# Who copies an attention group's last transposed probabilities, and where one row tile of the output projection begins

## The reference

```
q = rms_norm(layernorm(x));  k = rms_norm(ctx);  v = ctx          # 16 q heads, 4 k/v heads of width 32
scores = einsum('bgnqd,bgkd->bgnqk', rope(q), rope(k)) / sqrt(32)
attn = softmax(where(causal, scores, -1e30))
out = einsum('bgnqk,bgkd->bgnqd', attn, v)
x = x + out.reshape(B, T, C) @ w_out.T
x = x + ffn0(layernorm(x))
x = x + softmax(layernorm_rows(similarity(layernorm(x), ctx)))    # its parts run inside the next batch's attention
x = x + experts(layernorm(x))
```

## Time and profile before

| | us |
|---|---|
| median of 3 runs (1294.71 to 1297.57) | 1295.18 |
| the profiled execution | 1294.44 |
| its span | 1292.6 |
| busy in the span: PE, DVE, ACT, POOL | 1197.4 (93%), 736.1 (57%), 523.0 (40%), 444.1 (34%) |
| chain that ended last | PE 71%, DVE 14%, ACT 6%, DMA 3% |

### The profile page before, as it was taken

One profiled execution on the slowest core, in us unless ns is written; L12 is line 12 of the kernel. 1 busy time (PEld: TensorE's weight loads), 2 busy tenths in 40 slices (PEclk: granted clock), 3 DMA queues, 4 the chain that ended last, 5 costly groups with the idle time before them and its releaser, 6 DMA issues.

```text
span 1292.6 us, 19512 instructions
## 1 busy us (share of the span) xinstructions
PE 1197.4 (93%) x6575; PEld 866.9 (67%) x6575; DVE 736.1 (57%) x1498; ACT 523.0 (40%) x1189; POOL 444.1 (34%) x508
## 2 busy tenths in 40 slices
PE   4999999989999998999999899999899999999990
PEld 3667777667777766777776677777456666666650
DVE  7957665686788579677867967554712222222220
ACT  4865222775412278541227853222333323233320
POOL 1431233431123442113353211121165555555530
PEclk8999999999999999999999999999999999999995
DMA  8013230002232000323200012642789999999847
GB/s 294 2 68 107 98 107 34 1 1 110 100 138 102 35 1 12 120 78 138 102 34 1 34 69 78 238 171 75 306 254 357 358 348 356 342 345 351 228 55 141
DMA packets 45907, 187.04 MB, mean 145 GB/s; under 512 B 6717, under 2 KB 9789, under 8 KB 31365
## 3 DMA queue, kind: packets, MB, share of 16 engines
q1 hardware_dynamic: 30964, 146.18, 30.0%
q0 software_dynamic: 14864, 39.85, 13.6%
HBM read 155.31 MB, written 34.90 MB: 147 GB/s over the span
## 4 chain that ended last, share of the span: by engine, by line
PE 71%; DVE 14%; ACT 6%; DMA 3%; issue 2%; POOL 2%; DVEq 0%; SPq 0%; POOLq 0%; ACTq 0%
PE PS L2547 14%; PE PS L1971 10%; PE PS L1973 10%; PE PS L1972 10%; PE PS L2563 4%; ACT P L871 4%; DVE NM L1401 3%; PE PS L2567 3%; PE PS L2059 3%; PE PS L2078 2%; PE PS L2537 2%; PE PS L1990 2%; DMA WRAW<-in_ffn 2%; PE PS L2364 1%; PE PS L2363 1%
## 5 line engine op out<-in xcount | busy, mean ns | idle before, releaser
L2547 PE MATMUL PS<-WE,XGT 128*128 128x384 f32 x512 | 192.7, 499 | 1.5 <-DVE HM L1948 0.8
L698 POOL CAST HH<-HID 128x512 fp32r<-128x512 f32 x44 | 37.2, 846 | 330.4 <-DVE HID L1777 317.2
L997 ACT ACTIVATE WHI<-WRAW 128x1280 fp32r<-128x1280 f32 x44 | 56.1, 1274 | 223.9 <-DMA WRAW<-in_ffn 223.9
L1971 PE MATMUL PS<-XTH,WHI 128*128 128x512 f32 x352 | 141.1, 401 | 3.3 <-DVE WLO L1720 3.3
L871 ACT ACTIVATE P<-PS,NM 128x512 f32<-128x512 f32 (+3 forms) x256 | 131.8, 532 | 25.8 <-DVE NM L1401 24.8
L1973 PE MATMUL PS<-XTH,WLO 128*128 128x512 f32 x352 | 138.2, 393 | 0.0
L1972 PE MATMUL PS<-XTL,WHI 128*128 128x512 f32 x352 | 138.0, 392 | 0.0
L2547 PEld LDWEIGHTS PS<-WE,XGT 128*128 128x128 f32 x512 | 87.1, 190 | 56.7 <-issue 21.5
L1955 DVE COPY HMT<-PS 128x256 f32<-128x256 f32 x64 | 27.2, 425 | 163.8 <-PE PS L2556 163.8
L2059 PE MATMUL PS<-ident,P 128*128 128x128 f32 x640 | 94.6, 280 | 18.5 <-ACT P L871 8.4
L1401 DVE TENSOR_REDUCE NM<-PS 128x2 f32<-128x1024 f32 (+2 forms) x96 | 98.8, 1040 | 20.4 <-PE PS L1980 20.1
(11 more groups left out here) (337 smaller groups left out, 2696.1 us busy)
## 6 DMA issues: line engine op xcount, KB each, us to landing
WE<-in_we SPq DMA_DIRECT2D x64, 1152.0 KB, 8.1
WRAW<-in_ffn SPq DMA_DIRECT2D x44, 1060.0 KB, 4.9
acc<-HN SPq DMA_DIRECT2D x17, 256.0 KB, 7.0
XIN<-in_x SPq DMA_DIRECT2D x4, 1024.0 KB, 5.5
out<-X SPq DMA_DIRECT2D x4, 1024.0 KB, 4.5
out<-acc POOLq DMA_DIRECT2D x1, 4096.0 KB, 22.9
hx<-HN SPq DMA_DIRECT2D x3, 1152.0 KB, 4.5
CTX<-in_ctx SPq DMA_DIRECT2D x4, 256.0 KB, 2.8
```

Of the source, the lines that this page charges most:

```text
L997: act.activation(WHI[slot][:, 0:WD], WRAW[slot][:, 0:WD], ACT.Copy).then_inc(S["wg_hi"], 1)
L1971: pe.matmul(dst, a[0], b_[0], start=first, stop=False, **kw)
L2547: mm = pe.matmul(bank(2 + s % 2, 0, 2 * F1), XGT[s % 2][:, k, :], WE[s][:, k * 2 * F1:(k + 1) * 2 * F1], start=(k == 0), stop=(k == KC - 1))
```

## The change

The table of who copies what is altered, and the engines' programs with it:

- Tile 0 (all four heads) of every group is copied by ScalarE instead of VectorE, behind ScalarE's copies of tile 1 and the fifth stack.
- Tile 2, head 3 of groups 0 to 2 is copied by VectorE instead of ScalarE, behind head 2. In the last group VectorE made that copy already; there tile 2, head 0 goes from VectorE to ScalarE.
- In group 0 of the batches with a tail, the first query stack is copied by VectorE instead of ScalarE, and one row-statistics instruction (L1343) moves behind the tile-2 copies.
- In group 2 with a tail, ScalarE takes the exponentials of y row tile 2 behind the tile-2 copy instead of ahead of its score exponentials.
- In batches 1 to 3, TensorE does the first two head groups of row tile 1's projection inside the last group: three matmuls between the transposes of tile 1 and tile 0, three between the context transposes and the value product. It waits there for two split outputs.

```diff
@@ turning_order
-            order += [("P", g, 2, 0, 1, "d"), ("P", g, 2, 1, 1, "a")]
+            order += [("P", g, 2, 0, 1, "a" if g == G - 1 else "d"), ("P", g, 2, 1, 1, "a")]
...
-                order += [("stack", g + 1, 0, "d"), ("stack", g + 1, 1, "a")]
-            order += [("P", g, 2, 2, 1, "d"), ("P", g, 2, 3, 1, "d" if g == G - 1 else "a")]
+                order += [("stack", g + 1, 0, "d"), ("stack", g + 1, 1, "d" if tail and g == 0 else "a")]
+            order += [("P", g, 2, 2, 1, "d"), ("P", g, 2, 3, 1, "d")]
...
-            order += [("P", g, 0, 0, 4, "d")]
+            order += [("P", g, 0, 0, 4, "a")]
@@ ScalarE, attention
-                    if tail and g == 2:
-                        exp_y(2)
                     exps(a, g, 3)
                     if tail and g == 0:
                         normed_T("xT3", 1)
+                    if g == G - 1:
+                        turned(g, 2, 0)
                     turned(g, 2, 1)
+                    if tail and g == 2:
+                        exp_y(2)
...
                     exps(a, g, 4)
-                    if g < G - 1:
+                    if g < G - 1 and not (tail and g == 0):
                         stack(g + 1, 1, QST[0])
                     exps(a, g, 5)
-                    if g < G - 1:
-                        turned(g, 2, 3)
...
                     if g < G - 1:
                         stack(g + 1, 4, QST[3])
+                    turned(g, 0, 0, 4)
@@ VectorE, attention
-                    turned(g, 2, 0)
+                    if g < G - 1:
+                        turned(g, 2, 0)
...
                     if g < G - 1:
                         stack(g + 1, 0, KST)
-                    if rows_in:
-                        n = stats_x2(b, 3)
+                        if rows_in:
+                            stack(g + 1, 1, QST[0])
                     if sims:
                         peak(0)
                     turned(g, 2, 2)
-                    if g == G - 1:
-                        turned(g, 2, 3)
+                    turned(g, 2, 3)
+                    if rows_in:
+                        n = stats_x2(b, 3)
...
                     divisors(g)
-                    turned(g, 0, 0, 4)
@@ TensorE, attention (projected_out moves ahead of the loop, unchanged)
                     turn(g, 1, 2, 2)
                     if g < G - 1:
                         stack(g + 1, 4)
+                    if tail and g == G - 1:
+                        pe.wait_ge(S["oT_lo"], 1 + (G - 1) * a + 2)
+                        projected_out(1, 0, 1)
                     turn(g, 0, 0, 4)
...
                         context_T()
-                        if not tail:
+                        if tail:
+                            projected_out(1, 1, 2)
+                        else:
                             router_sums()
                     times_v(g)
...
-                    projected_out(t, 0, KC - 1)
+                    projected_out(t, 2 if tail and t == 1 else 0, KC - 1)
```

More of the change, by code:

```diff
@@ L881, in turned @@
                     src = bank(turns.bank("P", g, t, n0, nh), 0, nh * (t + 1) * P)
-                    src = src.rearrange("p (n j q) -> p n j q", n=nh, q=P) if nh > 1 else src.rearrange(
+                    src = src.rearrange("p (n j q) -> p n j q", n=nh, q=P) if t == 1 else src.rearrange(
                         "p (j q) -> p j q", q=P)
@@ L2170, in context_T, with projected_out @@
                     mm.then_inc(S["ctxT_ps"], 1)
+                def projected_out(t, k0, k1):
+                    sl = slice(t * P, (t + 1) * P)
+                    for k in range(k0, k1):
+                        mm = three(bank(2 + t), (OTH[:, k, sl], OTL[:, k, sl]), (woH[:, k, :], woL[:, k, :]),
+                                   k == 0, k == KC - 1)
+                    return mm
                 for g in range(G):
@@ L2230, in attention @@
                         keys_out()
-                def projected_out(t, k0, k1):
-                    sl = slice(t * P, (t + 1) * P)
-                    for k in range(k0, k1):
-                        mm = three(bank(2 + t), (OTH[:, k, sl], OTL[:, k, sl]), (woH[:, k, :], woL[:, k, :]),
-                                   k == 0, k == KC - 1)
-                    return mm
                 pe.wait_ge(S["oT_lo"], 1 + (G - 1) * (a + 1))
```

## The result

The changed kernel took 1283.99 us (median of 4 runs, 1283.72 to 1285.12), the kernel before beside it 1295.27 (1294.71 to 1297.57): a ratio of 0.9911, 95% interval 0.9894 to 0.9928, or 11.3 us less. The prediction was 1286.2 (1282.8 to 1291.5), faster. The profiled execution after took 1285.12 us with a span of 1283.3, which is 9.3 less than the span before. The forecast against the profiled execution was 9.0, but that these two agree so closely is chance, as the table shows: a start that came 1.4 later and a batch that gained 1.5 more than forecast nearly cancel.

The account below looks back on a forecast made before the run. TensorE bounds the FFN; in attention three engines hand over to each other, leaving short waits. 3 x (1.1 + 0.95 + 1.05) - 0.3 = 9.0 us off 1294.44 gives 1285.4, at the median 1286.2 (1282.8 to 1291.5).

Parts of the forecast that it names:

- Groups 0 to 1: Batches 1 to 3, transition from group 0: TensorE's waits for ScalarE copies go, scores start earlier; gain 1.1 us a batch.
- Groups 2 to 3: Batches 1 to 3: earlier transposes and VectorE maxima free of the tile-0 copy, staying early afterwards; gain 0.95 us a batch.
- Groups 1 to 2: Transition where VectorE waits for a similarity product: the extra copy ends just before it lands; 0 (0 to 0.1 lost).
- Projection: Last group, batches 1 to 3: six matmuls (1.4 us) saved behind the value product, 0.3 paid ahead; gain 1.05 a batch.
- Batch 0: First batch: VectorE's added copy meets GpSimd's subtraction; 0.6 and 0.2 us lost, group 2 gains 0.5; loss 0.3.
- more comes back: Rival: early projection partly fills the idle before batch 2's low TensorE clock; without the dip, with upper ends, 1283; chance 0.08.
- gain is cut: Rival: later gates in the group transitions of batches 1 to 3 take back part of the gain; 1290.1 us, chance 0.20.
- VectorE's row becomes the gate: Rival: copies added on VectorE delay the second stack copy in all transitions of batches 1 to 3; 1298.5 us, chance 0.05.
- The early step: Last group, batches 1 to 3: rival that transposes behind the early projection slip 0.7 us, leaving 0.4 a batch; 1288, no separate chance.

Follow-up runs that it names:

- e3: Kernel before with only the tile-2, head-3 copy of groups 0 to 2 moved to VectorE: 1290.89 us, ratio 0.9975.
- e4: Kernel before with only the tile-0 copy of every group moved to ScalarE: 1290.59 us, ratio 0.9974.
- e6: Changed kernel with the first query stack of group 0, batches 1 to 3, copied by ScalarE again: 1284.78 us.
- e9: Changed kernel without the early projection, three useless projection matmuls filling the idle ahead of the last group's tile-0 transposes in batches 1 to 3: 1286.60 us, ratio 0.9934.
- e1: Kernel before with only the early projection in the last group of batches 1 to 3, all copies as before: 1289.95 us, ratio 0.9967.
- e2: Changed kernel without the early projection, all copies moved: 1288.47 us, ratio 0.9960.
- e7: Changed kernel with batch 0's first query products on VectorE moved behind the second stack copy and the tile-1 copy, groups 0 and 1: 1282.55 us.
- e5: Changed kernel with batch 0's tile-2, head-3 copy of groups 0 and 1 given back to ScalarE: 1282.78 us.
- e8: Changed kernel with one more projection step inside the last group of batches 1 to 3, ahead of the tile-1 transposes: 1281.99 us.

## Why the prediction was right, point by point

- **Groups 0 to 1, 1.1 a batch:** measured 1.08, 1.10 and 1.06. Each gate on the way lay within 0.03 us of where the prediction put it. e3, e4 and e6 share it out: 0.47 for head 3, 0.12 for tile 0, 0.48 for the stack copy. The prediction named the XTF copy as the next gate; that is where the change stopped gaining.
- **Groups 2 to 3, 0.95 a batch:** 0.56 up to group 2's value product (forecast 0.6) and the rest behind it. In e9, where no projection blurs it, V2 to V3 is 0.50 shorter, and the stage of batch 1 is 2.00 shorter than before, 0.92 of it behind group 0. The claim that VectorE's row, once early, stays early to the last group's maxima held: ScalarE's wait of 1.47 us shrank to 0.46, and the exponentials of tile 1 came 0.91 earlier, counted from group 1's value product.
- **Groups 1 to 2, 0:** 23.13 and 23.12 in batch 1. In batch 2 it went from 23.46 to 23.11. This 0.35 was not foreseen. Both profiles of before and e1 have it, e2 and e4 don't, e3 has half; its cause was not followed.
- **Projection, 1.05 a batch:** saved behind 1.33 (forecast 1.4), paid ahead 0.24 in e1 and 0.38 in the changed kernel against e9 (forecast 0.3 to 0.4). For the whole stage, e1 against before gives 1.02 and 0.98 in batches 1 and 3, the changed kernel against e9 1.07, 0.97 and 0.78 in the three.
- **Batch 0, loss 0.3:** measured 0.27 at group 0 (0.2 forecast), 0.44 at group 1 (0.6), -0.74 at group 2 (-0.5), +0.18 in the last group (0, cause not followed): 0.15 in all. Group 1 was over-sized because the new copy runs beside the subtraction's first part, so the product was held for 0.72 us (1.41 - 0.69) where before it was 0.96 (1.65 - 0.69). Counted from group 0's value product, the stack copy came 0.48 later, not 0.65. The claim that the engines block each other stands: e7 moved the products away from the subtraction and they took 0.68 and 0.69. The section "Who interferes with whom" of the Trainium skill's page "SBUF — State Buffer" has a VectorE instruction with two SBUF inputs contend with a GpSimd instruction that reads SBUF, and here the trace agrees with it.
- **The sum:** with batch 1's figures, 3 x (1.08 + 0.92 + 1.07) - 0.15 = 9.1 against 9.0. So the steps that the prediction counted came out as it had them. What it did not count is worth 1.5 us in the profiles (next point), and the median, 1283.99, lies 2.2 under the forecast of 1286.2: inside the range, but right at the lower edge of the band from 1284 to 1289 that had 0.62.
- **What was under-weighed:** the clock. The prediction saw the low clock of the earlier trace rows behind a 0.74 us wait that the projection partly fills, and gave the rival "more comes back" 0.08, as if it were as likely to appear elsewhere. Its dip should have stood in the main case: the same idle stands in all three batches, and filling it took the low clock out of the last groups of every profile. (It appeared elsewhere in e5 and e7, once each, at 0.4 to 0.5 us.) Each occurrence in a last group costs 0.9 to 1.3 us, 1.18 in the profile of before. That, with the 0.35 in batch 2, is 1.5 us; at the median the kernel gained 11.3 with an interval from about 9.3 to 13.7 (10.7 against the mean of the later medians of before, 1294.7). 9.1 + 1.5 = 10.6 accounts for it within what these runs can tell.
- **The other rivals:** "gain is cut" put the scores of group 3 at 0.4 earlier and VectorE's maxima held; the maxima came 0.92 earlier. "VectorE's row becomes the gate" happened in batch 0 alone, where its idle ahead of the stack copy was nil, which is the point the prediction gave for it. Its own sum is 0.3 off: batch 0 with nothing gained at group 2 is 0.6 + 0.2 = 0.8 lost, not 1.1, which gives 1298.2. The early step fitted its gap.

## What to carry to other kernels

When three engines hand over in a ring, price a moved copy by walking the gates: write down which copy releases each step, shift it, and find the next copy that is late. Counted that way from the timeline of before, the chains of batch 1 came out to within 0.1 us at every gate. In batch 0, where two engines hold each other up, three of the four groups were some 0.2 off. Ask in each short idle whether work from behind can stand there: its worth was the work (1.05 a batch) and the clock on top. And look at the engine that takes the copy in every variant of the loop: VectorE had room in the batches with a tail and none in batch 0, where the same edit costs 0.7.

## What the runs showed of the hardware

- TensorE's clock dropped to its lower level behind a run of short waits (1.15, 0.26 and 0.74 us in e2; 0.98, 0.26 and 0.74 in the kernel before), came back after some 3 us, and cost 0.9 to 1.3 us each time. It dropped in 5 of 15 such places, and in none of 24 where the last of the waits was filled, even with matmuls whose result nobody reads. Waits of 1.22, 0.23 and 0.58 us in the router of the last batch had it in 3 of 13 profiles. A faster kernel can so be a slower one: e2's last group came sooner and took 1.2 us longer.
- The first group of batch 0 takes longer when TensorE has less than its full clock from 20 to 30 us. With the same program for batch 0 it took 18.19 us at 1.00 (e6), 18.72 at 0.83 (e9), and 18.87 and 19.03 at 0.67 (the changed kernel and e8). The first scores start between 21.70 and 24.09 us. Spans of single profiles differ by that, so periods inside a stage are the measure.
- A VectorE product with two SBUF inputs is held until a GpSimd subtraction with SBUF inputs is through (1.65 and 1.41 us instead of 0.69, and 0.68 and 0.69 again once moved behind it), while a VectorE copy from PSUM that runs beside the subtraction keeps its 0.56 us.
